# A token-routed expert kernel: its token table and shared expert in another order

## The reference

```python
logits = xt @ router_w.T                       # T = 2048 tokens, E = 64
probs = softmax(logits)
top_w, top_i = top_k(probs, 8);  top_w = top_w / sum(top_w)
comb[t, top_i] = top_w
routed = sum over e of comb[:, e:e+1] * ((silu(xt @ Wg[e].T) * (xt @ Wu[e].T)) @ Wd[e].T)
shared = sigmoid(xt @ Wse.T) * ((silu(xt @ Wsg.T) * (xt @ Wsu.T)) @ Wsd.T)
return routed + shared                         # F = 128 hidden columns in each expert
```

## Time and profile before

| what | value |
|---|---|
| time, median of 3 runs | 1165.45 us (1163.73 to 1166.33) |
| the profiled execution | 1166.61 us |
| its span, first to last instruction | 1164.8 us |
| mean granted TensorE clock | 0.978 |
| TensorE, VectorE, ScalarE, POOL busy | 1068.5, 668.9, 505.4, 610.8 us |
| indirect gathers and scatters on POOL | 159 and 157 |

### The profile page before, as it was taken

How to read it: one execution, slowest core, us unless ns; L and a number is a source line. 1 busy time by engine, 2 the same in 40 slices (tenths; PEclk the granted TensorE clock), 3 DMA queues, 4 the chain that set the end, 5 groups by cost and what they waited for, 6 DMA issues and landing times.

```text
span 1164.8 us, 24407 instructions
## 1 busy us (share of the span) xinstructions
PE 1068.5 (92%) x6269; PEld 721.7 (62%) x6270; DVE 668.9 (57%) x2306; ACT 505.4 (43%) x1421; POOL 610.8 (52%) x634
## 2 busy tenths in 40 slices
PE   5999899899999979988869999999999999999954
PEld 3655566555566545655547777776777776767721
DVE  5666566556666668867644544554444444444448
ACT  3666576566666644446622222222222222222224
POOL 4434333333333313321148888887888887788810
PEclk9999999999999999989989999999999999999988
DMA  9700000000000052100169989999999999998788
GB/s 318 290 2 1 3 1 1 2 2 1 1 2 2 1 202 79 55 28 19 56 205 215 221 199 252 245 233 232 253 234 250 240 236 264 269 222 172 118 274 324
DMA packets 66279, 166.73 MB, mean 143 GB/s; under 512 B 15378, under 2 KB 17170, under 8 KB 66080
## 3 DMA queue, kind: packets, MB, share of 16 engines
q0 software_dynamic: 38496, 83.95, 33.0%
q1 hardware_dynamic: 27712, 81.88, 19.8%
HBM read 119.85 MB, written 62.65 MB: 157 GB/s over the span
## 4 chain that ended last, share of the span: by engine, by line
PE 74%; DMA 12%; DVE 6%; issue 4%; ACT 2%; POOL 1%; DVEq 0%; SPq 0%; POOLq 0%; ACTq 0%
PE ps L971 16%; PE ps L710 15%; PE ps L982 8%; PE ps L769 7%; DMA sum_rows<-x_t,idx 6%; DMA x_t<-x_rows,idx 5%; PE ps L827 4%; PE ps L955 4%; PE ps L739 4%; PE ps L789 4%; PE ps L863 2%; PE ps L724 2%; PE ps L879 2%; PE ps L843 1%; PE ps L977 1%
## 5 line engine op out<-in xcount | busy, mean ns | idle before, releaser
L971 PE MATMUL ps<-big,work 128*128 x1264 | 300.1, 380 | 0.0
L464 POOL DMA_INDIRECT sum_rows<-x_t,idx x157 | 249.9, 1592 | 55.8 <-issue 45.7
L971 PEld LDWEIGHTS ps<-big,work 128*128 128x128 f32 x1264 | 228.7, 191 | 24.8
L458 POOL DMA_INDIRECT x_t<-x_rows,idx x159 | 166.2, 1045 | 58.7 <-issue 31.7
L710 PE MATMUL ps<-big 128*128 128x384 f32 x512 | 179.2, 493 | 2.1 <-ACT big L528 1.7
L664 ACT ACTIVATE work<-ps 128x512 f32<-128x512 f32 x159 | 95.0, 597 | 188.0 <-PE ps L955 136.3
L384 POOL TENSOR_TENSOR work<-qkv_all,rope_sb 128x256 f32<-128x256 f32 x64 | 46.8, 730 | 241.9 <-ACT qkv_all L533 241.9
L982 PE MATMUL ps<-big,work 128*128 x314 | 160.9, 594 | 1.8 <-issue 1.7
L955 PEld LDWEIGHTS ps<-ident_sb,x_t 128*128 128x128 f32 x636 | 78.1, 142 | 107.4 <-issue 73.9
L1076 DVE CUSTOM_DVE_ANT_0 ps<-ps,mask_sb 128x128 f32<-128x128 f32 (+3 forms) x256 | 120.6, 513 | 24.1 <-PE ps L739 23.4
L552 ACT ACTIVATE work<-ps,neg_max 128x128 f32<-128x128 f32 (+3 forms) x256 | 132.5, 528 | 3.3 <-DVE neg_max L1076 2.4
(11 more groups left out here) (183 smaller groups left out, 1444.9 us busy)
## 6 DMA issues: line engine op xcount, KB each, us to landing
big<-experts SPq DMA_DIRECT2D x65, 768.0 KB, 14.2
sum_rows<-x_t POOLq DMA_DIRECT2D x4, 2048.0 KB
big<-sum_rows SPq DMA_DIRECT2D x8, 768.0 KB, 9.5
x_rows<-work SPq DMA_DIRECT2D x16, 256.0 KB, 2.0
sum_rows<-attn_t POOLq DMA_DIRECT2D x2, 2048.0 KB
out<-x_sb SPq DMA_DIRECT2D x16, 256.0 KB, 5.8
x_sb<-x SPq DMA_DIRECT2D x3, 1024.0 KB, 9.6
x_t<-sum_rows SPq DMA_DIRECT2D x4, 768.0 KB, 13.0
```

The source lines that it names most:

```text
L458: pool.indirect_dma_start(rows[:, q, :], None, x2_rows, bass.IndirectOffsetOnAxis(ap=idx[:, q, 0:1], axis=0), bounds_check=last_row, oob_i ...
L464: pool.indirect_dma_start(all_sums, bass.IndirectOffsetOnAxis(ap=idx[:, q, 1:2], axis=0), y_sb[:, q, :], None, bounds_check=last_sum, oob_ ...
L971: mm = pe.matmul(ps[:, 2 + p, 0:GATEUP], rows_t[:, p, c, :], w_ring[:, slot, c * GATEUP:(c + 1) * GATEUP], start=(c == 0), stop=(c == DC - 1))
```

## The change

The shared expert's tiles are split: 13 (EARLY) run with the table, and the last three (LATE) stand after it, among the first gathers and the loop's first products. Half of the row spread and `shared_up(0)` (into bank 6) move up between the last products of the projection stage; the count then comes ahead of `shared_up(1)`. Within a tile a group of table products now stands between turn and down (FILL_A), and in six tiles a second one after the down (FILL_B), so that all 16 groups are done in tiles 3 to 12. VectorE makes the first two groups of one-hots ahead of the expert tables. POOL's masking and scaling move to tiles 7 and 8. The three late tiles' hidden product is VectorE's (`shared_late`), straight from PSUM. The token table is finished in two parts, its first eight columns first, and the first seven gathers read it directly. The shared rows go to DRAM in three parts (tiles 0 to 5, 6 to 10, 11 to 15), the last of which POOL issues behind the gathers. Buffers are laid out anew so that the late tiles' input outlives the first gathers. The diff, cut:

```diff
+LATE = 3
+EARLY = TILES - LATE
+HEAD = DEEP + 2
+FILL_A = {3: 0, 4: 1, 5: 3, 6: 4, 7: 6, 8: 8, 9: 9, 10: 11, 11: 12, 12: 14}
+FILL_B = {4: 2, 6: 5, 7: 7, 9: 10, 11: 13, 12: 15}
...
+        rows = [x2_t[:, q // 2, q % 2 * XROW:(q % 2 + 1) * XROW] for q in range(DEEP)]
+        y_sb = [x2_t[:, DC - 1, q * D:(q + 1) * D] for q in range(DC - 1)] + \
+            [x2_t[:, c, (DC - 1) * D:DC * D] for c in range(DEEP - DC + 1)]
...
+            for r in range(NW - 1):
+                sp.wait_ge(s_wl[r], 16)
+                sp.sem_inc(s_ready, 1)
             sp.wait_ge(s_sdn, TILES)
             sp.dma_start(w_ring[:, NW - 1, :], experts[NW - 1]).then_inc(s_wl[NW - 1], 16)
-            for r in range(NW):
-                sp.wait_ge(s_wl[r], 16)
-                sp.sem_inc(s_ready, 1)
+            sp.wait_ge(s_wl[NW - 1], 16)
+            sp.sem_inc(s_ready, 1)
...
+            def keep_shared(lo, hi, done):
+                pool.wait_ge(s_sy, hi)
+                pool.dma_start(sums_v[0][:, lo:hi, :], y_shared[:, lo:hi, :]).then_inc(done, 16)
+            for i in range(EARLY):
...
-                if i == 1:
+                if i == 7:
...
-                if i == 3:
+                if i == 8:
...
-            for half in range(2):
-                pool.wait_ge(s_sy, 8 * half + 8)
-                pool.dma_start(sums_v[0][:, 8 * half:8 * half + 8, :],
-                               y_shared[:, 8 * half:8 * half + 8, :]).then_inc(s_scatter[0], 16)
-
...
+                if i == 9:
+                    keep_shared(0, 6, s_scatter[0])
+            def gather(q, at):
...
             pool.wait_ge(s_combd, 16)
-            pool.wait_ge(s_sht, TILES)
-            pool.wait_ge(s_shte, TILES)
             pool.wait_ge(s_tables, 4)
             full = pool.value_load(pairs_i[0:1, 0:1], min_val=(B * S * K // P + DEEP - 2) // DEEP - 1,
                                    max_val=(HIGH + DEEP - 2) // DEEP - 1)
+            keep_shared(6, 11, s_ysh)
+            pool.wait_ge(s_sgu, EARLY)
+            pool.wait_ge(s_head, 1)
             for t in range(DEEP + 1):
-                pool.wait_ge(s_idx, t + 1)
                 if t >= DEEP:
                     pool.wait_ge(s_xg_ps, t - DEEP + 1)
                     pool.wait_ge(s_weight, t - DEEP + 1)
-                gather(t % DEEP)
+                gather(t % DEEP, token_i[:, t:t + 1])
+            keep_shared(11, TILES, s_scatter[0])
+            pool.wait_ge(s_ysh, 16)
             def pass_tile(j, c, gathers):
                 t = j * DEEP + (c + 1)
                 if gathers:
-                    pool.wait_ge(s_idx, t + (DEEP + 1))
+                    pool.wait_ge(s_idx, t)
                     pool.wait_ge(s_xg_ps, t + 1)
                     pool.wait_ge(s_weight, t + 1)
                     pool.sem_inc(s_issue, 1)
-                    gather((c + 1) % DEEP)
+                    gather((c + 1) % DEEP, idx[:, (c + 1) % DEEP, 0:1])
...
+            def shared_gate(i):
+                act.wait_ge(s_sgu, i + 1)
+                bank = ps[:, 6 if i == 0 else 2 + i % 2, 0:GATEUP]
+                if i < EARLY:
                     if i >= 2:
                         act.wait_ge(s_shid, i - 1)
...
+            shared_gate(0)
+            for i in range(1, EARLY):
+                shared_gate(i)
+                shared_hidden(i - 1)
+                if i in FILL_B:
+                    steps_of(FILL_B[i])
+                shared_y(i - 1)
+                if i == 2:
+                    act.wait_ge(s_step_at, 1)
+                if i + 1 in FILL_A:
+                    steps_of(FILL_A[i + 1])
+                if i == 8:
+                    act.wait_ge(s_tables, 4)
+                    quads = act.value_load(pairs_i[0:1, 1:2], min_val=(B * S * K // P + DEEP - 2) // DEEP, max_val=(HIGH + DEEP - 2) // DEEP)
...
+            shared_gate(13)
+            shared_hidden(12)
+            shared_gate(14)
+            shared_y(12)
+            shared_hidden(13)
+            shared_gate(15)
             turned(0, 0)
+            shared_y(13)
+            shared_hidden(14)
             turned(1, 1)
+            shared_y(14)
+            act.wait_ge(s_late, LATE - 1)
             silu(0, 0)
+            shared_hidden(15)
             turned(2, 0)
+            shared_y(15)
+            act.wait_ge(s_late, LATE)
...
             def shared_up(i):
+                bank = ps[:, 6 if i == 0 else 2 + i % 2, 0:GATEUP]
+                if 2 <= i < EARLY + 2:
                     pe.wait_ge(s_up, i - 1)
+                if i >= EARLY + 2:
+                    pe.wait_ge(s_late, i - EARLY - 1)
                 if i == 0:
                     pe.wait_ge(s_ws, 16)
-                    pe.wait_ge(s_x2t, TILES)
+                if i < 2:
+                    pe.wait_ge(s_x2t, 1 if i == 0 else TILES)
...
             def tile_rows():
                 pe.wait_ge(s_cnt, 2)
-                pe.matmul(tables[0:1, 96:96 + HIGH], ones_sb[0:E, 0:1], past_end, start=True, stop=True).then_inc(s_row_ps, 1)
+                pe.wait_ge(s_step_at, 1)
+                pe.matmul(ps[0:1, 0, 0:HIGH], ones_sb[0:E, 0:1], past_end, start=True, stop=True).then_inc(s_row_ps, 1)
...
-            for i in range(TILES + 1):
+            for i in range(TILES + 3):
                 if i < TILES:
+                    project(i)
+                if i >= 3:
+                    route(i - 3)
+                if 2 <= i < TILES + 2:
+                    turn_x2(i - 2)
+                if i == TILES:
+                    spread_rows(0)
+                if i == TILES + 1:
+                    shared_up(0)
+            spread_rows(1)
+            count_rows()
+            shared_up(1)
+            place_rows()
+            for i in range(1, EARLY):
+                if i >= 2:
                     shared_up(i)
-                if i == 0:
-                    spread_rows(0)
-                    count_rows()
-                    spread_rows(1)
-                    place_rows()
-                if i >= 1:
-                    shared_turn(i - 1)
-                if i == 2:
+                shared_turn(i - 1)
+                if i == 3:
                     tile_rows()
-                if i >= 1:
-                    shared_down(i - 1)
-                if i >= 4 and i < TILES:
-                    fill_table(i - 4)
-            for n in range(TILES - 4, TILES):
-                fill_table(n)
+                if i in FILL_A:
+                    fill_table(FILL_A[i])
+                shared_down(i - 1)
+                if i in FILL_B:
+                    fill_table(FILL_B[i])
...
-            pe.wait_ge(s_table, 1)
             pe.sem_inc(s_dn, 1)
+            pe.wait_ge(s_tables, 4)
             quads = pe.value_load(pairs_i[0:1, 1:2], min_val=(B * S * K // P + DEEP - 2) // DEEP, max_val=(HIGH + DEEP - 2) // DEEP)
+            load_slots(0)
+            shared_up(13)
+            shared_turn(12)
+            shared_up(14)
+            shared_down(12)
+            shared_turn(13)
+            shared_up(15)
             turn_rows(0, 0, 16)
-            load_slots(0)
+            shared_down(13)
+            shared_turn(14)
             turn_rows(1, 1, 16)
+            shared_down(14)
+            pe.wait_ge(s_late, LATE - 1)
             up(0, 0, slot_of(0))
+            shared_turn(15)
             turn_rows(2, 2, 16)
+            shared_down(15)
+            pe.wait_ge(s_shte, TILES)
             turn_hidden(0, 0)
+            pe.wait_ge(s_late, LATE)
             up(1, 1, slot_of(1))
+            pe.wait_ge(s_sy, TILES)
...
+            def one_hots(n):
...
+            one_hots(0)
+            one_hots(1)
...
+            for n in range(2, 12):
+                one_hots(n)
+            quads = dve.value_load(pairs_i[0:1, 1:2], min_val=(B * S * K // P + DEEP - 2) // DEEP, max_val=(HIGH + DEEP - 2) // DEEP)
+            for n in range(12, TILES):
+                one_hots(n)
+            def tokens(lo, hi):
...
             dve.wait_ge(s_masked_e, 1)
...
             dve.wait_ge(s_one_used, TILES * K)
...
+            tokens(0, HEAD).then_inc(s_head, 1)
+            step(tokens(HEAD, HIGH))
             dve.memset(token_i[:, HIGH:COLS], NOWHERE).then_inc(s_table, 1)
 
-            dve.wait_ge(s_table, 1)
-            dve.wait_ge(s_tables, 4)
...
+            def shared_late(i):
+                dve.wait_ge(s_silu, i + 1)
+                if i >= 2:
+                    dve.wait_ge(s_sht, i - 1)
+                dve.tensor_tensor(out=hidden[:, i % 2, :], in0=gate[:, i % 2, :], in1=ps[:, 2 + i % 2, F:GATEUP],
+                                  op=ALU.mult).then_inc(s_late, 1)
...
-            for t in range(DEEP):
-                stage_gather(t, t)
+            shared_late(13)
+            dve.wait_ge(s_table, 1)
+            shared_late(14)
             weight(0, 0, 16)
-            stage_gather(DEEP, 0)
+            shared_late(15)
+            dve.wait_ge(s_sht, TILES - 1)
             hide(0, 0)
+            dve.wait_ge(s_sdn, TILES - 1)
```

(54 more changed lines are left out.)

93 lines of the change are left out of this document (33 added, 60 removed).

## The result

The changed kernel takes 1158.56 us (median of six runs, 1157.12 to 1160.86), the kernel before, on the same chip, 1166.69: a ratio of 0.9932 with an interval of 0.9913 to 0.995, so 8.1 us faster. The forecast was 12.7 faster, 1152.7, with a range up to 1158.5. The profiled execution took 1158.39, its span is 1156.6.

What follows compares the result with a forecast made beforehand. The moment of POOL's first scatter was taken to set the end, with the loop unchanged at 506.5 us. Moving it from 605.6 to 592.8 took 12.8 off 1166.61, giving 1153.8, or 1152.7 as median; range 1147 to 1158.5.

Steps and rivals of the forecast that it cites:

- What sets the end: At the loop's start: the moment of POOL's first scatter moves the whole loop and the tail behind it.
- Start of the one-hots: VectorE ahead of the table: one-hots begin at 519.7, from 522.6 minus 2.2 (masking moved) and 0.7 (earlier count).
- One-hots: Table stage: VectorE is the bound, its stream sums to 48.4, last product at 568.4, table's end 18.3 earlier.
- Hand-over: From table to loop: register loads, 15.4 of late work and 1.2 for clock put the first down at 587.7, 15.1 earlier.
- What is late next: Before POOL's first scatter: it waits for shared rows 11 to 15, landing at 592.8, so comes 12.8 earlier.
- The loop keeps 506.5: First to last scatter: instructions and DMAs keep number and size, so the loop stays at 506.5 us.
- The sum: Whole kernel: profiled 1166.61 minus 12.8 is 1153.8; the median of the runs, 1.16 lower, gives 1152.7.
- shared rows free: Before the first scatter: last shared rows land before 590.5, the end follows the first down, 1150.4; chance 0.13.
- clock: TensorE stays at half clock in the front (+3) and through more late tiles (+2), 1157.7; chance 0.16.
- TensorE's pace: Table stage: locks cost nothing or little and the load is hidden, table ends at 562.5, 1146.7; chance 0.13.
- the other side: One-hots: VectorE slows beside ScalarE and TensorE; no gain from 3.3 us a group, 1168.7 at 3.5; chance 0.05.
- it doesn't do what it says: Loop: it takes the gain back, its pace being the DMA engines', not POOL's queue's; 1165; chance 0.05.

Runs made afterwards that it cites:

- Gate freed: Last shared rows (tiles 11 to 15) go to the third table of sums, not the first, against the changed kernel; 1154.71 us, ratio to before 0.9886.
- front undone: Half of the row spread and the first shared up product go back behind the last router product, against the changed kernel; 1161.94 us.
- weights held back: SP issues slot 7's weights only after the last shared rows have landed, against the changed kernel; 1154.52 us.
- late rows doubled: Shared rows of tiles 6 to 15 go to DRAM in one piece, 2.62 MB in place of 1.31, against the changed kernel; 1161.66 us.

## Why the prediction was partly wrong

**What sets the end: right.** Gate freed moved the first scatter and left TensorE alone, and the end went with POOL.

**Start of the one-hots: right in sum.** 519.7 was forecast; 521.3 less 2.44 is 518.9, and 520.2 in the second profile. The slot step takes 0.23, as forecast, with POOL's masking gone from beside it; the front pieces were counted at 0.7 and bring some 2.4. The rest brings less than the 2.2 counted: with the front undone the first one-hot is at 100.4, 1.5 ahead of the 101.9 that is the mean of before.

```profile
520.22 0.23 DVE L1299 TENSOR_SCALAR slot_i<-work 128x128 int32<-128x128 f32 x1
```

**One-hots: right in sum, with one wrong term.** The last product was forecast for 568.4; it ended at 569.48, less 2.44 is 567.0. The load was counted at 1.3 and costs nothing. The masks were counted at 3.8 and cost 3.6. Rows of the changed kernel's VectorE show both; the one-hots beside the masks with the first of these, and one beside a hidden product:

```profile
541.93 2.35 POOL L462 TENSOR_TENSOR wo_sb<-wo_sb,qkv_all 128x1024 f32<-128x1024 f32 x1
541.97 2.37 DVE L1314 TENSOR_SCALAR low<-count_h,work,token_sb 128x128 f16<-128x128 f16 x1
...
550.52 1.92 DVE L1314 TENSOR_SCALAR low<-count_h,work,token_sb 128x128 f16<-128x128 f16 x1
...
562.20 0.49 DVE L1317 TENSOR_SCALAR low<-count_h,work 128x128 f16<-128x128 f16 x1
```

The last is 0.49 in place of 0.24, so a hidden product of 0.46 costs 0.25, as forecast. The rule of the Trainium skill weighed in the prediction ("SBUF — State Buffer", section "SBUF: two separate sides") fits the long rows, where a one-hot lasts about as long as POOL's operation; its full 0.46 per hidden product would be too much here, as the trace shows.

**Hand-over: right by cancelling.** The first down was forecast for 587.7; 590.1 less 2.44 is 587.7. That the four errors cancel is luck. The idle time was 3.3 for 2.7 and the clock 2.5 for 1.2, paid for by the table's 1.4 and a late list of 14.9 for 15.4 (572.76 to 590.13, less 2.5).

**What is late next: this step failed, by size.** The mechanism was named, the term too small. The issue was forecast for 586.8 and came at 587.0 (589.48 less 2.44). The landing was forecast 6.0 behind it and came 8.2 behind it, and POOL's scatter 0.8 after that, which the prediction left out altogether: 9.0 from issue to scatter in place of 6.0, and 8.0 to 9.0 in the seven profiles with this transfer as it is. So the first scatter moved by 9.5 (184.3 to 174.8) rather than 12.8. The prediction put the landing between 591.9 and 594.0, by bytes over a rate. It counted the 1.31 MB and half of the weights' 0.79, but not the gather that POOL issues at 590.70 (128 rows of 576 float32, 0.29 MB). The three are 2.39 MB, and that is what was moved from issue to landing (8.18 us at 292 GB/s). Nor did it have a term for the end of the transfer: in the windows the engines move 333 to 419 GB/s from 590 to 596 and some 50 from 596.5 to 597.66. With the weights held back, issue to scatter still took 7.3.

The Trainium skill, "DMA: Bandwidth & Descriptors", section "Anatomy of one DMA — SWDGE (gpsimd) path", gives a fixed 2 us and the bytes over 436 GB/s, estimates of 5.0 for 1.31 MB and 8.0 for 2.62 MB alone. Measured beside the weights and the gather were 8.2 and 10.8: the step between the two, 2.6 against 3.0, is near. The level is not: with the bytes of the other two transfers added the estimates are 7.5 and 10.5, still 0.7 and 0.3 short.

**The loop keeps 506.5: right as a mechanism, not to the microsecond.** It was 506.5 and 505.1 in the two profiles of before, and 501.1 to 507.1 in the twelve others, 503.6 in the mean; eleven of these twelve are shorter than both of before. So some 2 us may belong to the change. No run isolates that.

**The sum.** From the profile of before to that after, the span fell by 8.2: the first scatter -9.5, the loop -2.4, the tail behind the last scatter +1.3, the start of the stage +2.4. Against the 12.8 forecast, 3.3 are the scatter's term. Of the absolute error of 5.9, another 1.2 is that before itself measured 1166.69 this time. The rest, 1.3, is within what the start and the loop vary by, and stays open. Of the rivals "shared rows free" describes the kernel with the gate freed, in its mechanism and not in its time (1150.4 against 1154.71); "clock" took part, with 1.3 more than forecast at the late tiles. "TensorE's pace", "the other side" and "it doesn't do what it says" are out: the table ended at 567, VectorE kept its pace (0.62 for the one-hots of two products, also in the middle of the stream), and the loop gave nothing back.

## What to carry to other kernels

When a stage gets shorter, follow the first instruction of the queue that sets the end to every semaphore it waits for, and cost each of those transfers to its landing and the wake behind it. Everything that was hidden under the old wait, such as a write of results, a weight load or a register load on TensorE, becomes a serial term, and a short idle stretch of TensorE can be paid a second time through its clock. Add up the bytes of every transfer that is in flight beside the one waited for, small ones too. Judge a small edit by landmarks measured from a common point just ahead of it: here one reordering looked like a gain of 1 us and was a loss of about 2 once the register loads were out of the way.

## What the runs showed of the hardware

What a register load costs depends on what stands behind it. On VectorE 1085 ns of it left no gap in the stream; on TensorE two loads at the hand-over were 3.28 us of idle time, and the same two among the table products took nothing that shows at the table's end.

Its own length varies as well. TensorE's first load took 1089 to 1139 ns in the nine profiles in which the DMA engines' share beside it was 0.90 to 1.02, and 492 to 499 in the five in which it was 0.00. The idle stretch at the hand-over was 3.19 to 3.29 in the seven changed kernels of the first kind, and 1.50 and 1.72 in the two of the second that still load there. That the DMA traffic is the cause was not tested by itself, and one load speaks against it: VectorE's, in the run with it late, took 597 ns at 571.5 with the engines' share at 1.02.

The clock behind such a stretch is not given by the stretch. Behind 3.2 to 3.3 us of idle time the next up took 2.79 to 3.75 in place of 1.73 (in the changed kernel at a granted clock of 0.58 and then 0.74), behind 1.50 it took 3.60, behind 1.72 it took 1.97.

The loop's length varies through a few long steps. POOL's step is 3.25 in the median, and each of the fourteen profiles has one to seven steps above 3.35, most of them in other places each time. What these add is 0.2 us in the shortest loop (501.1) and 4.5 in the longest (507.1), so they are the larger part of the difference, not all of it. The longest step is in the run with late rows doubled, in POOL's timeline, and then in its chain of waits:

```profile
996.83 1.05 POOL L472 DMA_INDIRECT x_t<-x_rows,idx  x1 [0.30 <-issue]
1000.07 1.60 POOL L478 DMA_INDIRECT sum_rows<-x_t,idx  x1 [2.19 <-issue]
```

```profile
990.32 10.13 DMA x_t<-x_rows,idx
1000.45 0.04 issue
1000.50 0.66 PE ps L1007 x4
```

A gather took 10.1 us to land, with the DMA engines at a share of 0.92 to 1.10, TensorE waited 1.46 for it, and the scatter was 1.9 late. POOL had nothing to make it up with. That the other long steps have this cause was not followed up.
